# Gram correction of a cross-attention kernel in 9 instead of 12 matmuls per group

## The chip, the cores and the metric

The kernel runs on one core of one Trainium2 chip. The metric is the device time of one execution in microseconds (us), taken as the median of several runs. The core has five engines with queues of their own: TensorE (PE, matrix products), VectorE (DVE), ScalarE (ACT), GpSimd (POOL) and SyncE (SP, which issues DMAs). They meet only at semaphores.

## The reference, cut to what matters

```python
B, S, C = 8, 112, 320; H, Dh = 20, 16          # batches, queries, channels; heads
text, ip = ctx[:, :371], ctx[:, 371:]          # 371 text tokens and 4 image tokens of 512 values
q = heads(x @ W_q); k = heads(text @ W_k); v = heads(text @ W_v)
P = softmax(q k^T / 4)                         # (8, 20, 112, 371)
text_out = P v
qsem = l2norm(P @ text)                        # a vector of 512 per head and query
sem  = qsem @ l2norm(ip)^T
p_ip = softmax(q k_ip^T / 4 + 0.5 * sem) * mask
out  = (text_out + p_ip v_ip) @ W_out + b_out + x
```

The length of `P @ text` is never computed over the 512 values. With G = text text^T (371 x 371) its square is p^T G p, so the kernel needs, for all 20 heads and 112 queries of a batch, the product of G with the exponentials. All of it must come out in float32 quality, while TensorE is run in a fast 32-bit mode ("f32r") that rounds its operands. So an operand is split into a high part that survives the rounding and a low part that holds the rest, and both are multiplied.

## The kernel before, in words

**Tiles.** The 371 text tokens are three blocks of 128, 128 and 115. A batch has five groups of four heads, 40 groups in all; a group's exponentials are three tiles of 128 x 448 (tokens by 4 x 112 queries).

**One batch's own work on TensorE** (units of the order): `K` c: the keys, three pieces, 12, 12 and 8 matmuls. `G` i: block row i of G, that is the diagonal block and what is to the right of it, 12 matmuls each of 376, 248 or 120 columns. `V` j: the values, 12 matmuls each. `max` h (`m`): one matmul of scores with queries on the partitions, for the maximum over tokens by head. `mT`: the 20 maxima, transposed; they go through DVE and three small DMAs back to the queries (`qst`), and `St` of the next batch waits for those.

**Work per group g.** `St` g c (`S0`, `S1`, `S2`): scores of block c into `P`; ScalarE takes the exponential into `big` and then a rounded copy of it into `er`. `gram` g j (`g2`, `g1`, `g0`, together `g`): G times `er` for block column j into `Y`, i from 0 to j, each with a matmul of the high part `Gh` and one of the low part `Gl`: 6 + 4 + 2 = 12 matmuls of 448 columns. The blocks above the diagonal are stored doubled, so that those below can be left out (p^T G p is symmetric). DVE multiplies each `Y` with the exponentials into `pb`, POOL adds the three up. `pv` g (`v`): exponentials times values, and the sum over tokens of those products.

**Buffers that set the order.** `Y` has two banks. Its three uses per group alternate, so `g0` can start only when DVE has multiplied `g2` of the same group (semaphore `s_P`). All of `K`, `G`, `V`, `max`, `mT`, `T`, `pT`, `cT`, `o` write into a ring `PR` of three banks: the n-th such unit waits until the (n-3)-th is read (`s_free0` to `s_free2`, which count for each bank what DVE or ScalarE have read). Where a unit `max` waits in DVE's queue, its bank and TensorE's third unit behind it wait too.

**What sets the order.** `master_schedule` writes one list of units by hand; every engine walks the same list and takes from it what concerns it, DVE through `behind`, which moves some units behind the next maximum or product. `ROUNDS` holds the five rounds in which batch b's groups run beside batch b+1's `K`, `G`, `V` and maxima; `EARLY` is the same for batch 0 and `LAST` for batch 7.

Before, a `G` unit goes: ScalarE copies the diagonal block and, times 2, the rest into `Gh` (L658, L661) and the four image columns into `Vt` (L665); DVE subtracts to get `Gl` (L799, L801), which frees the bank. All matmuls but transposes carry line L905.

## Time and profile before

| | |
|---|---|
| median of 3 runs | 412.04 us (411.01 to 414.87) |
| the profiled execution, its own time | 411.41 us |
| its span, first to last instruction | 409.6 us |
| TensorE busy | 393.6 us, 96% of the span |
| VectorE busy | 220.2 us, 54% |
| ScalarE busy | 206.0 us, 50% |
| GpSimd busy | 206.3 us, 50% |
| TensorE clock granted, mean | 0.997 of full speed |

Matmuls overlap in the records: each is shown from its first column in to its last column out, so a row's duration is longer than the time for which it holds the engine. That time is the distance between the starts of two rows.

### The profile page before, as it was taken

How to read it: one execution, taken by the hardware profiler on the slowest of the kernel's cores; microseconds unless marked ns; L12 is line 12 of the kernel's file. 1: busy time of each engine (PE TensorE's matmuls, PEld its weight loads, DVE VectorE, ACT ScalarE, POOL GpSimd, SP SyncE). 2: the span in 40 equal slices, each digit the busy share in tenths (PEclk: the TensorE clock that was granted, in tenths of full speed). 3: DMA queues.
4: the chain of work that ended last, by engine and by line, in shares of the span. 5: the costliest groups of instructions: out<-in, count | busy, mean ns of one | idle time of the engine just before them, and what ended most of it. 6: DMA issues, size and time to landing. Idle time of an engine off the chain costs nothing.

```text
span 409.6 us, 9494 instructions
## 1 busy us (share of the span) xinstructions
PE 393.6 (96%) x3653; PEld 319.5 (78%) x3653; DVE 220.2 (54%) x482; ACT 206.0 (50%) x484; POOL 206.3 (50%) x218
## 2 busy tenths in 40 slices
PE   7999799899899999999999999999999999999995
PEld 4648688678788878888789878887888878876762
DVE  0795764575267534665366526663556646643432
ACT  1534134555645565555556564456455366458722
POOL 3020361262527872576437662687247443844981
PEclk9999999999999999999999999999999999999998
DMA  8499994338204802273207511470208210001000
GB/s 259 140 292 234 213 172 84 92 126 166 75 2 150 145 14 72 75 161 61 82 6 193 97 49 36 146 144 18 72 2 168 51 40 2 3 3 39 3 16 15
DMA packets 29455, 38.03 MB, mean 93 GB/s; under 512 B 14361, under 2 KB 26745, under 8 KB 28729
## 3 DMA queue, kind: packets, MB, share of 16 engines
q1 hardware_dynamic: 28514, 36.36, 37.0%
q10 hardware_dynamic: 896, 1.07, 0.9%
q8 instruction: 29, 0.48, 0.5%
q14 instruction: 16, 0.13, 0.1%
HBM read 28.50 MB, written 8.81 MB: 91 GB/s over the span
## 4 chain that ended last, share of the span: by engine, by line
PE 88%; DVE 3%; ACT 2%; issue 2%; DMA 2%; POOL 1%; POOLq 0%; SPq 0%; ACTq 0%; DVEq 0%
PE PR L905 42%; PE Y L905 27%; PE P L905 10%; PE O L905 8%; DMA pb<-wq 1%; DVE big L773 1%; PE PR L1063 1%; ACT big L681 1%; ACT er L685 1%; POOL pb L547 1%; DVE mx L807 1%; DMA qst<-ma 0%; POOLq L169 0%; SPq L460 0%; ACT cTs L729 0%
## 5 line engine op out<-in xcount | busy, mean ns | idle before, releaser
L547 POOL TENSOR_TENSOR pb<-pb 128x448 f32<-128x448 f32 x78 | 89.1, 1142 | 110.4 <-DVE pb L829 104.9
L807 DVE TENSOR_REDUCE mx<-PR 112x1 f32<-112x371 f32 x160 | 83.7, 540 | 78.1 <-PE PR L905 77.1
L905 PE MATMUL Y<-er,Gh 128*128 128x448 f32 x240 | 95.3, 397 | 1.7 <-ACT er L685 0.8
L829 DVE TENSOR_TENSOR pb<-big,Y 128x448 f32<-128x448 f32 x120 | 72.6, 621 | 39.2 <-PE Y L905 39.0
L905 PE MATMUL Y<-er,Gl 128*128 128x448 f32 x240 | 87.3, 364 | 0.0
L681 ACT ACTIVATE big<-P 128x448 f32<-128x448 f32 x120 | 65.2, 543 | 18.7 <-PE P L905 17.9
L685 ACT ACTIVATE er<-big 128x448 fp32r<-128x448 f32 x120 | 69.3, 578 | 3.8
L905 PEld LDWEIGHTS Y<-er,Gh 128*128 128x128 f32 x240 | 45.1, 188 | 13.7 <-DVE pb L829 9.1
L905 PE MATMUL PR<-kst,qst 96*112 96x371 bf16 x160 | 51.3, 331 | 2.2 <-DVE mx L807 2.0
L905 PEld LDWEIGHTS Y<-er,Gl 128*128 128x128 f32 x240 | 45.2, 188 | 2.1
L905 PE MATMUL P<-qst,kst 99*128 99x112 bf16 x480 | 42.0, 214 | 1.5 <-ACT big L681 1.1
L905 PEld LDWEIGHTS P<-qst,kst 99*128 99x128 bf16 x480 | 29.8, 99 | 17.0 <-issue 8.0
L649 ACT ACTIVATE ks<-PR 128x372 bf16<-128x372 f32 (+1 forms) x24 | 10.3, 429 | 47.8 <-PE PR L905 47.2
L905 PE MATMUL PR<-wvh,eh 128*128 128x320 f32 (+1 forms) x96 | 32.3, 336 | 0.2 <-ACT Vt L673 0.2
L673 ACT ACTIVATE Vt<-PR 128x320 f32<-128x320 f32 (+1 forms) x24 | 10.6, 442 | 41.2 <-PE PR L905 41.2
L905 PE MATMUL O<-big,Vt 128*22 128x112 f32 x960 | 31.0, 262 | 0.0
L905 PE MATMUL PR<-eh 128*128 128x376 f32 (+2 forms) x96 | 29.7, 310 | 0.0
L905 PE MATMUL PR<-wvl,eh 128*128 128x320 f32 (+1 forms) x96 | 29.7, 309 | 0.0
L905 PE MATMUL PR<-wvh,el 128*128 128x320 f32 (+1 forms) x96 | 29.6, 309 | 0.0
L569 POOL TENSOR_TENSOR t<-ssq,halfm 112x20 f32<-112x20 f32 (+2 forms) x9 | 28.8, 3202 | 1.4 <-DVE ssq L845 1.3
L905 PE MATMUL PR<-eh,el 128*128 128x376 f32 (+2 forms) x96 | 28.0, 292 | 0.0
L905 PE MATMUL PR<-el,eh 128*128 128x376 f32 (+2 forms) x96 | 28.0, 292 | 0.0
(154 smaller groups left out, 653.5 us busy)
## 6 DMA issues: line engine op xcount, KB each, us to landing
et<-ctxT SPq DMA_DIRECT2D x8, 752.0 KB, 4.4
kst<-kd SPq DMA_DIRECT2D x7, 720.0 KB, 7.2
kd<-ks SPq DMA_DIRECT2D x16, 288.0 KB, 2.9
qst<-qd SPq DMA_DIRECT2D x48, 70.0 KB, 2.4
...
```

Source lines behind the costliest of these rows:

```text
L547: pool.tensor_tensor(total, total, (pz, pm)[j], ALU.add).then_inc(s_S, 1)
L569: power = pool.tensor_tensor(t1[:, hs], ssq[:, hs], halfm[:, hs], ALU.pow)
L649: act.activation(ks[:, 0, TP * c:TP * c + w], bank[:, 0:w], ACT.Copy).then_inc(s_kh, 1)
L673: act.activation(Vt[b % 2][0:r, i, :, 0:D], bank[0:r, 0:C].rearrange("p (h d) -> p h d", d=D), ACT.Copy).then_inc(s_free[seq[u] % NR], 1)
L681: act.activation(e, P[(3 * g + c) % 2][:, 0:448], ACT.Exp).then_inc(s_exp, 1)
L685: act.activation(er[g % 2][:, 448 * c:448 * c + 448], e, ACT.Copy).then_inc(s_er, 1)
L773: dve.tensor_tensor(kblk[0:w, c, :, :].rearrange("p b (h n) -> p b h n", n=NIP), src, m, ALU.mult).then_inc(s_kb, 1)
L807: dve.tensor_reduce(mx[b % 2][:, h:h + 1], bank[0:S, 0:T], AX.X, ALU.max).then_inc(s_free[seq[u] % NR], 1)
L829: dve.tensor_tensor((pz, pm, pa[g % 2])[j], eb[g % 3][:, 448 * j:448 * j + 448], Y[y % 2][:, 0:448], ALU.mult).then_inc(s_P, 1)
L905: return pe.matmul(o, st, mv, start=start, stop=stop, **kw)
L1063: last = pe.transpose(bank[0:S, 128 * (r - lo):128 * (r - lo) + 128], OT[b % 2][:, r, :], ident[:, :])
```

## The change

G is no longer stored as it is. With c the diagonal element of a token's row and 1/c its reciprocal, row i of the stored matrix is divided by c, and the exponential's copy `er` is multiplied by c (ScalarE, `scale=gc`). Of a diagonal block only the half above the diagonal is kept, twice, with 1/2 (times 2) on the diagonal, which is exact after the division. The low parts of that upper half are transposed on TensorE (new unit `D` i, L1031) and put below the diagonal of the same block of `Gh`. So a diagonal block needs one matmul per product where it had two, 5 + 3 + 1 = 9 for a group. `Gl` is left for the blocks right of the diagonal.

DVE's part of a `G` unit is now a chain of six instructions that wait for each other (L828 to L834: diagonal, its lower bound, reciprocal, upper half, its remainder, remainder times c), then `Gl` once ScalarE has copied the rest (L841), and one more (L850) when the transposed piece is back. ScalarE starts on a `G` unit only behind `s_gd`, near the chain's end, and from batch 2 on it takes its part of `G` behind the next exponential (`late_g`). The bank of `G` is free after L841. `usel` is 2 instead of 1, and the DMA of the 128 x 128 identity becomes one of 128 x 384 (identity and two triangular masks), queued ahead of the image tokens' loads.

The rounds are written anew: two maxima stand between `K0` and `g` of the first, none between `S0` and `g` of the others; `V1` comes as the fourth ring unit behind the fourth group's products; the last maximum stands right before `mT`. Before batch 0, `G` and `K` of the next batch alternate.

```diff
+LOFF = (0, 256)
+TINY = 1e-30
...
-ROUNDS = ("S0 K0 m g m K1 S1 m v S2 m G0 m",
-          "S0 m g m K2 m S1 v m S2 G1 m",
-          "S0 m g2 T0 T1 g1 g0 m r0 G2 m S1 m pw v S2 m V0",
-          "Kr S0 r1 m g m V1 m S1 m m v r2 S2 mT z V2",
+ROUNDS = ("S0 K0 m m g m S1 m v S2 m K1 m G0",
+          "S0 g m S1 m v D0 S2 K2 m G1 m",
+          "S0 g m S1 T0 T1 v r0 m D1 S2 m G2 pw m V0",
+          "Kr S0 r1 g m D2 S1 m V1 m m v r2 m S2 m mT z V2",
           "p E g pT v cT S0 S1 o S2")
 EARLY = ("m S0 m K1 g m S1 m S2 m",
-         "S0 m g m S1 K2 m S2 v m m",
-         "S0 m g m S1 m v S2 V0 m m",
-         "Kr S0 m g m V1 m S1 m m v S2 mT V2",
+         "S0 m g m S1 K2 m S2 v D0 m m",
+         "S0 m g m S1 m v D1 S2 V0 m m",
+         "Kr S0 m g m D2 V1 m S1 m m v S2 mT V2",
...
-    order += [("G", 0, i) for i in range(3)] + [("K", 1, c) for c in range(3)] + [("Kr", 1)]
-    side = [("V", 0, 0), ("V", 0, 1), ("V", 0, 2)] + [("qip", b) for b in range(B)]
+    order += [u for c in range(3) for u in (("G", 0, c), ("K", 1, c))] + [("Kr", 1)]
+    side = [u for c in range(3) for u in (("V", 0, c), ("D", 0, c))] + [("qip", b) for b in range(B)]
...
-        if u[0] in ("K", "G") and u[1] >= 2:
+        if u[0] == "K" and u[1] >= 2:
             out, held = out + held, [u]
+        elif u[0] == "G":
+            out, held = out + held + [u], [("Gl",) + u[1:]]
         else:
             out.append(u)
-            if u[0] in ("max", "gram", "mT", "o"):
+            if u[0] in ("max", "gram", "mT", "o", "K"):
                 out, held = out + held, []
     return out + held
 
 
-RING = ("K", "G", "V", "T", "pT", "cT", "o", "max", "mT")
+def late_g(order):
+
+    out, held = [], []
+    for u in order:
+        if u[0] == "G" and u[1] >= 2:
+            held.append(u)
+        else:
+            out.append(u)
+            if u[0] == "St":
+                out, held = out + held, []
+    return out + held
+
+
+RING = ("K", "G", "D", "V", "T", "pT", "cT", "o", "max", "mT")
...
                 elif k == "G":
                     b, i, r = u[1], u[2], ROWS[u[2]]
-                    filled(act, u)
+                    act.wait_ge(s_gd, 3 * b + i + 1)
                     if b == 0:
                         act.wait_ge(s_set, FILLS)
                     if b >= 2:
                         act.wait_ge(s_gram, 3 * NG * (b - 1))
-                    a = min(128, T - 128 * i)
-                    act.activation(Gh[b % 2][0:r, GOFF[i]:GOFF[i] + a], bank[0:r, 0:a], ACT.Copy)
-                    rest = T - 128 * i - a
+                    rest = T - 128 * i - r
                     if rest:
-                        act.activation(Gh[b % 2][0:r, GOFF[i] + a:GOFF[i] + a + rest], bank[0:r, a:a + rest],
-                                              ACT.Copy, scale=2.0)
+                        act.activation(Gh[b % 2][0:r, GOFF[i] + r:GOFF[i] + r + rest], bank[0:r, r:r + rest],
+                                       ACT.Copy, scale=grc[b % 2][0:r, i:i + 1])
                     if b >= 2:
                         act.wait_ge(s_pv, NG * (b - 1))
...
-                    act.activation(er[g % 2][:, 448 * c:448 * c + 448], e, ACT.Copy).then_inc(s_er, 1)
+                    act.activation(er[g % 2][:, 448 * c:448 * c + 448], e, ACT.Copy,
+                                   scale=gc[g // NG % 2][:, c:c + 1]).then_inc(s_er, 1)
...
+                        dve.wait_ge(s_mk, 16)
+                    if b >= 2:
+                        dve.wait_ge(s_gram, 3 * NG * (b - 1))
+                    filled(dve, u)
+                    c, rc = gc[b % 2][0:r, i:i + 1], grc[b % 2][0:r, i:i + 1]
+                    low, diag = dj[i][0:r, 0:r], Gh[b % 2][0:r, GOFF[i]:GOFF[i] + r]
+                    link(dve.scalar_tensor_tensor(low, bank[0:r, 0:r], 1.0, ident[0:r, 0:r], ALU.mult, ALU.mult, accum_out=c))
+                    link(dve.tensor_scalar(c, c, TINY, None, ALU.max))
+                    link(dve.reciprocal(rc, c))
+                    link(dve.scalar_tensor_tensor(diag, bank[0:r, 0:r], rc, half_upper[0:r, 0:r], ALU.mult, ALU.mult))
+                    dve.scalar_tensor_tensor(low, bank[0:r, 0:r], rc, diag.bitcast(f32), ALU.mult, ALU.subtract).then_inc(s_gd, 1)
+                    dve.wait_ge(s_gd, 3 * b + i + 1)
+                    dve.scalar_tensor_tensor(low, low, c, upper[0:r, 0:r], ALU.mult, ALU.mult).then_inc(s_ru, 1)
+                elif k == "Gl":
+                    b, i, r = u[1], u[2], ROWS[u[2]]
+                    n = seq[("G", b, i)]
+                    o, rest = GOFF[i], T - 128 * i - r
                     dve.wait_ge(s_gh, 3 * b + i + 1)
-                    gh, gl = Gh[b % 2], Gl[b % 2]
-                    a = min(128, T - 128 * i)
-                    rest = T - 128 * i - a
-                    o = GOFF[i]
-                    low = dve.tensor_tensor(gl[0:r, o:o + a], bank[0:r, 0:a], gh[0:r, o:o + a].bitcast(f32), ALU.subtract)
                     if rest:
-                        low = dve.scalar_tensor_tensor(gl[0:r, o + a:o + a + rest], bank[0:r, a:a + rest], 2.0,
-                                                       gh[0:r, o + a:o + a + rest].bitcast(f32), ALU.mult, ALU.subtract)
-                    low.then_inc(s_free[seq[u] % NR], 1)
+                        dve.scalar_tensor_tensor(Gl[b % 2][0:r, LOFF[i]:LOFF[i] + rest], PR[n % NR][0:r, r:r + rest],
+                                                 grc[b % 2][0:r, i:i + 1], Gh[b % 2][0:r, o + r:o + r + rest].bitcast(f32),
+                                                 ALU.mult, ALU.subtract).then_inc(s_free[n % NR], 1)
+                    else:
+                        dve.sem_inc(s_free[n % NR], 1)
+                elif k == "D":
+                    b, i, r = u[1], u[2], ROWS[u[2]]
+                    filled(dve, u)
+                    diag = Gh[b % 2][0:r, GOFF[i]:GOFF[i] + r]
+                    dve.scalar_tensor_tensor(diag, bank[0:r, 0:r], grc[b % 2][0:r, i:i + 1], diag.bitcast(f32), ALU.mult,
+                                             ALU.add).then_inc(s_free[seq[u] % NR], 1)
...
+                elif k == "D":
+                    b, i, r = u[1], u[2], ROWS[u[2]]
+                    pe.wait_ge(s_ru, 3 * b + i + 1)
+                    if b == 0 and i == 0:
+                        pe.wait_ge(s_mk, 16)
+                    pe.transpose(bank[0:r, 0:r], dj[i][0:r, 0:r], ident[0:r, 0:r]).then_inc(s_ring, 1)
...
-                        freed(pe, seq[("G", b, 2)])
+                        for i in range(3):
+                            freed(pe, seq[("D", b, i)])
                     if j == 2:
                         pe.wait_ge(s_er, 3 * g + 3)
                     d = Y[y % 2][:, 0:448]
                     for i in range(j + 1):
                         o = GOFF[i] + 128 * (j - i)
                         mv = er[g % 2][:, 448 * i:448 * i + 448]
-                        mm(d, Gh[b % 2][:, o:o + 128], mv, i == 0, False)
-                        last = mm(d, Gl[b % 2][:, o:o + 128], mv, False, i == j)
+                        last = mm(d, Gh[b % 2][:, o:o + 128], mv, i == 0, i == j)
+                        if i < j:
+                            o = LOFF[i] + 128 * (j - i - 1)
+                            mm(d, Gl[b % 2][:, o:o + 128], mv, False, False)
                     last.then_inc(s_gram, 1)
                 elif k == "pv":
                     g = u[1]
```

**DVE, batch 2 on, second round.** What DVE does between the maximum (`mx`) ahead of the second `G` unit and the group's first two products (`pb`). Before:

```order
L807 TENSOR_REDUCE mx<-PR 112x1 [waits s_ring]
L799 TENSOR_TENSOR Gl<-PR,Gh 128x128 [waits s_gh]
L801 SCALAR_TENSOR_TENSOR Gl<-PR,Gh 128x115
L807 TENSOR_REDUCE mx<-PR 112x1 [waits s_ring]
L829 TENSOR_TENSOR pb<-big,Y 128x448 [waits s_pv,s_gram]
```

Now:

```order
L828 SCALAR_TENSOR_TENSOR dj,gc<-PR,masks 128x128 [waits s_kres,s_ring,s_gram]
L829 TENSOR_SCALAR gc<-gc 128x1 [waits s_d]
L830 RECIPROCAL grc<-gc 128x1 [waits s_d]
L831 SCALAR_TENSOR_TENSOR Gh<-PR,grc,masks 128x128 [waits s_d]
L832 SCALAR_TENSOR_TENSOR dj<-PR,grc,Gh 128x128 [waits s_d]
L834 SCALAR_TENSOR_TENSOR dj<-dj,gc,masks 128x128 [waits s_gd]
L855 TENSOR_REDUCE mx<-PR 112x1 [waits s_ring]
L841 SCALAR_TENSOR_TENSOR Gl<-PR,grc,Gh 128x115 [waits s_gh]
L877 TENSOR_TENSOR pb<-big,Y 128x448 [waits s_pv,s_gram]
```

Two instructions for `G` have become seven, and all seven stand ahead of the first product.

**TensorE, batch 2 on, fourth round,** from the last product of the group (the `Y` row that waits for `s_P`) to the second `V` unit. Before:

```order
L905 MATMUL Y<-er,Gh 128x448 [waits s_P]
L905 MATMUL Y<-er,Gl 128x448
L905 MATMUL PR<-kst,qst 112x371 [waits s_free2]
L905 MATMUL PR<-wvh,eh 128x320 [waits s_free0]
```

Now:

```order
L953 MATMUL Y<-er,Gh 128x448 [waits s_P]
L953 MATMUL PR<-kst,qst 112x371 [waits s_free2]
L1031 MATMUL PR<-masks,dj 115x115 [waits s_ru,s_free0]
L953 MATMUL P<-qst,kst 128x112 [waits s_exp]
L953 MATMUL P<-qst,kst 128x112 x3
L953 MATMUL PR<-kst,qst 112x371 [waits s_free1]
L953 MATMUL PR<-wvh,eh 128x320 [waits s_free2]
```

`V` (the row with `wvh,eh`) now needs bank 2, which the maximum right behind the products fills; before it needed a bank that was filled ahead of them.

**TensorE, the end of the fourth round,** from the third of the scores to the transpose of the maxima (`mx`). Before:

```order
L905 MATMUL P<-qst,kst 128x112 [waits s_exp]
L905 MATMUL P<-qst,kst 128x112 x3
L1000 MATMUL PR<-ident,mx 20x112 [waits s_free0,s_free1]
L905 MATMUL PR<-wvh,eh 115x320 [waits s_free2]
```

Now:

```order
L953 MATMUL P<-qst,kst 128x112 [waits s_exp]
L953 MATMUL P<-qst,kst 128x112 x3
L953 MATMUL PR<-kst,qst 112x371 [waits s_free0]
L1055 MATMUL PR<-masks,mx 20x112 [waits s_free0,s_free1]
L953 MATMUL PR<-wvh,eh 115x320 [waits s_free2]
```

One maximum has moved between the scores and the transpose that needs it.

## Rows read from the trace of the kernel before

**Rows 1.** The page: busy time, share of span, instructions; chain that ended last.

```profile
PE 393.6 (96%) x3653; PEld 319.5 (78%) x3653; DVE 220.2 (54%) x482; ACT 206.0 (50%) x484; POOL 206.3 (50%) x218
...
PE 88%; DVE 3%; ACT 2%; issue 2%; DMA 2%; POOL 1%; POOLq 0%; SPq 0%; ACTq 0%; DVEq 0%
PE PR L905 42%; PE Y L905 27%; PE P L905 10%; PE O L905 8%; DMA pb<-wq 1%; DVE big L773 1%; PE PR L1063 1%; ACT big L681 1%; ACT er L685 1%; POOL pb L547 1%; DVE mx L807 1%; DMA qst<-ma 0%; POOLq L169 0%; SPq L460 0%; ACT cTs L729 0%
```

**Rows 2.** Timeline of TensorE, one group's products: start us, us, instruction [idle before].

```profile
200.26 0.50 PE L905 MATMUL Y<-er,Gh 128*128 128x448 f32 x1
200.60 0.36 PE L905 MATMUL Y<-er,Gl 128*128 128x448 f32 x1
...
201.40 0.36 PE L905 MATMUL Y<-er,Gl 128*128 128x448 f32 x1
...
202.48 0.47 PE L905 MATMUL Y<-er,Gh 128*128 128x448 f32 x1
202.79 0.36 PE L905 MATMUL Y<-er,Gl 128*128 128x448 f32 x1
202.99 0.32 PE L905 MATMUL PR<-kst,qst 96*112 96x371 bf16 x1
```

**Rows 3.** Timeline of DVE, the same group.

```profile
200.59 0.54 DVE L807 TENSOR_REDUCE mx<-PR 112x1 f32<-112x371 f32 x1 [2.12 <-PE PR L905]
201.06 0.53 DVE L780 TENSOR_TENSOR kr<-PR,ks 128x372 f32<-128x372 f32 x1
201.80 0.62 DVE L829 TENSOR_TENSOR pb<-big,Y 128x448 f32<-128x448 f32 x1 [0.21 <-PE Y L905]
202.60 1.21 DVE L829 TENSOR_TENSOR pb<-big,Y 128x448 f32<-128x448 f32 x2 [0.17 <-PE Y L905]
```

**Rows 4.** Chain of waits in order of time: start us, us, what, instructions.

```profile
205.74 0.90 PE O L905 x32
...
218.94 0.54 PE PR L1063 x5
...
228.63 2.08 PE PR L905 x14
```

**Rows 5.** Timeline of DVE, instructions that do and don't wait for each other.

```profile
37.51 0.28 DVE L799 TENSOR_TENSOR Gl<-PR,Gh 128x128 fp32r<-128x128 f32 x1
37.71 0.40 DVE L801 SCALAR_TENSOR_TENSOR Gl<-PR,Gh 128x243 fp32r<-128x243 f32 x1
...
233.07 0.26 DVE L815 SCALAR_TENSOR_TENSOR mr<-PR,ma 20x112 f32<-20x112 f32 x1
233.37 0.20 DVE L817 CAST ma<-mr 20x112 bf16<-20x112 f32 x1
```

**Rows 6.** Timeline of ScalarE around a `G` unit.

```profile
217.57 0.25 ACT L665 ACTIVATE Vt<-PR 128x80 f32<-128x80 f32 x1
217.69 0.56 ACT L681 ACTIVATE big<-P 128x448 f32<-128x448 f32 x1
218.28 0.58 ACT L685 ACTIVATE er<-big 128x448 fp32r<-128x448 f32 x1
...
225.71 0.44 ACT L673 ACTIVATE Vt<-PR 128x320 f32<-128x320 f32 x1 [0.77 <-PE PR L905]
```

**Rows 7.** Timeline before batch 0, DVE.

```profile
35.80 1.79 DVE L747 TENSOR_TENSOR el<-et,eh 128x752 fp32r<-128x752 f32 x2 [2.61 <-ACT eh L630]
...
46.18 3.96 DVE L773 TENSOR_TENSOR big<-kipT,hq 128x640 f32<-128x640 f32 x3
```

**Rows 8.** Timeline before batch 0, TensorE.

```profile
50.64 0.81 PE L905 MATMUL PR<-kst,qst 96*112 96x371 bf16 x2 [1.84 <-DVE mx L807]
...
62.80 0.36 PE L905 MATMUL PR<-kst,qst 96*112 96x371 bf16 x1
63.89 0.26 PE L1000 MATMUL PR<-ident,mx 112*20 112x112 f32 x1 [0.73 <-DVE mx L807]
```

**Rows 9.** Busy time by stretch: PE, PEld, DVE, ACT, POOL, clock, DMA share, GB/s.

```profile
4.00:8.00 4.00, 2.67 (x11) 2.04 (x10) 0.00 (x0) 0.16 (x1) 0.70 (x6) 1.00 0.99 277
...
405.00:409.60 4.60, 1.03 (x3) 0.39 (x3) 0.49 (x1) 0.26 (x1) 0.00 (x0) 0.77 0.10 31
```

30 lines of the change are left out of this document (22 added, 8 removed).

## The prediction, made before the changed kernel ran

> **What bounds the kernel now.** I read the page first: TensorE is busy 96% of the span and the chain that ended last is TensorE to 88%, of which the products into `Y` are 27% [rows 1]. So matmuls taken out should shorten it, unless TensorE then waits instead. The next view is the timeline of one group's products on TensorE [rows 2] beside DVE's [rows 3]. Matmuls follow at 0.20 us (200.60 to 201.40 is four steps), so twelve would take 2.40 us. The block takes 2.59: from its effective start at 200.40 to 202.99. The missing 0.19 is one stall: the third product (`g0`) starts at 202.48 because the multiply that empties its `Y` bank ran 201.80 to 202.42. TensorE is already at the edge of waiting for DVE inside each group, although DVE is busy only 54%. The reader should keep one number from here: the distance from the last `g2` matmul's start (201.40) to the release of `g0` (202.42) is 1.02 us, all DVE and latency, and the change doesn't shorten it.
>
> **Matmuls removed.** 40 groups lose 3 of 12. With 5 + 3 + 1, the last `g2` matmul starts 0.20 earlier, so DVE's multiply ends at 202.22 and `g0` starts at 202.28; it is one matmul, and the next unit starts 0.31 later (202.48 to 202.79 [rows 2]), at 202.59 instead of 202.99. A group gains 0.40 us, not 0.60: a third goes into a longer wait for `Y`. 40 x 0.40 = 16.0; in batch 7 the scores stand between the products and cover some 0.1 of the wait in each of 5 groups: **-16.5 us**.
>
> **Transposes added.** 24 `D` units. Five transposes of 128 x 128 take 0.54 us on the chain [rows 4], 0.11 each: **+2.6 us**.
>
> **DVE's chain for a `G` unit.** No row has it, so I bound it. Instructions that wait for each other start 0.30 us apart for 0.26 of work; two that don't start 0.20 apart for 0.28 [rows 5]. The chain is six: four on a 128 x 128 tile, two on a column. Lower end: all at 0.20, 1.2 us. Upper end: all at 0.32, 1.9. I take 1.55 (four at 0.29, two at 0.20), nearest the rows that wait. The Trainium skill (VectorE: DVE Perf Modes, The DRAIN you can't avoid) says that a semaphore between two DVE instructions costs nothing extra. By that rule the chain would be near 1.2 and the sum some 5 us lower; the rows above speak against it.
>
> What this costs depends on what stands behind it. I walked batch 4's five rounds in the new order, with these steps: maximum 0.16 us on TensorE and 0.46 on DVE (200.59 to 201.06 [rows 3]), multiply 0.60, `pv` 0.90 [rows 4], `V` 1.76 (2.08 less two maxima [rows 4]), scores 0.20, exponential and copy together 1.15 on ScalarE [rows 6]. Let the products start at S; DVE must have multiplied `g2` by S+1.82.
>
> - Round 1: DVE has two maxima and `K`'s remainder (3 x 0.46) at its queue's head when the products start, and comes 0.2 late. **0.2 us.**
> - Round 2: `G0` ends 0.2 before S, DVE's chain runs S+0.0 to S+1.5, the multiply ends at S+2.1. **0.3.** (Chain 1.2: nothing.)
> - Round 3: `G1` and a maximum end 0.2 before S; DVE does the chain to S+1.4, the maximum to S+1.85, `Gl` to S+2.05, then the multiply to S+2.65. **0.8.** (Chain 1.2: 0.5; 1.9: 1.15.)
> - Round 4, ScalarE: it takes `G2` behind the exponential of `S0`, and DVE's multiply stands behind `s_gh`. `V0` ends at S-0.2; ScalarE does `Vt` (0.44), exponential and copy (1.15), then 0.25 [rows 6], done near S+1.7; the multiply ends at S+2.3. **0.5**, whatever the chain takes.
> - Round 4, ring: behind the products come maximum, `D2`, scores, maximum, `V1`, and `V1` needs the first one's bank. Let X be the end of the `g2` multiply. TensorE is there at X+1.0 (0.37 to leave `g0`, 0.16, 0.11, 0.20, 0.16). DVE first does two multiplies (1.2), then the maximum (0.54): X+1.8. **0.8.** Before, `V1` used a bank filled ahead of the products.
> - Round 4, the last maximum: it stands right ahead of `mT`. From a maximum's start to such a transpose's start is 1.09 us where nothing else is between (62.80 to 63.89 [rows 8]; the chain puts it at 1.02 behind the matmul's own start-up), against 0.16 for the maximum. **0.85.** Before, `pv` and the scores lay between.
> - Round 5: nothing new, **0**.
>
> 3.45 us in each of batches 1 to 6, the rounds that carry `G` and `D`: **+20.7 us**. In batch 0's rounds `G` is done before and `V1` waits for an older bank: only the gains above.
>
> **Before batch 0.** (a) `K` of batch 1 now stands second, but DVE's split of its context ends at 37.59 (35.80 + 1.79 [rows 7]), while `G0` ends near 35.9: TensorE idles 1.65 us. (b) In the alternation the fourth unit needs `G0`'s bank, which is free after chain 1.55, ScalarE's 0.6, and, on DVE, `K`'s remainder and `Gl`: about 1.3 more for both such places, less what (a) covered, so the first `V` starts 2.9 us late. (c) DVE then builds a block of 3.96 us [rows 7]. Before, `V1` ran beside it and TensorE idled 1.84 [rows 8]; now a third maximum stands ahead of `V1`, the ring is full earlier, and V1's 1.76 come behind: +1.2 net of the later start. Together **+4.1**. (d) Batch 1's three `G` units follow on each other with three chains (4.65 us) and three `Gl`; here ScalarE takes `G` in the old place, so the first exponential waits about 2.9 us longer, and the first products start 2.0 later: **+2.0**.
>
> **Costed at nothing.** The mask DMA moves 128 KB more, 0.5 us at the 277 GB/s of its stretch [rows 9], ahead of image-token loads that are used near 30 us. Three small fills on POOL lie before any use; POOL's sums wait for DVE anyway. ScalarE's copies keep their count and size (the scale comes from a column); if that costs 0.05 each, 6 us on an engine half idle. The way of the maxima from `mT` to the next scores takes 5.0 us; between them stand `V2`, the products, `pv` and, in batches 1 to 4, `cT`: 5.5 us or more, so it stays hidden by half a microsecond.
>
> **Sum.** -16.5 + 2.6 + 20.7 + 6.1 = +12.9. Of this I take 2 off: the chain has 2% "issue" [rows 1], 8 us of small gaps, some of which lie under the new waits. The profiled execution took 411.4 us, 0.6 under the median of 412.0; so 412.0 + 10.9 = **423 us**.
>
> **Rivals.**
> 1. *DVE keeps up and the matmuls' time is collected: faster.* One mechanism: at each group TensorE's queue holds work that needs neither the ring nor `Y`, and the waits I found vanish. For it: DVE has 190 us idle now and gets about 40 more of work; the new rounds put the scores and two maxima elsewhere. Against: the listed places are fixed orders in a ring of three. It decides by one number: the fixed parts sum to -16.5 + 2.6 + 6.1 = -7.8, so below 1.3 us of waits in a batch it is faster, above it slower. With 0.5 a batch: 412 - 7.8 + 3 = 407 us; without the prologue's delay 402. Chance of more than 1% faster: 0.14.
> 2. *Half of the waits.* With a chain of 1.2 us and the round-1 and round-2 waits gone, or the ring's wait halved, 1.7 to 2 us a batch are left and 4 before batch 0: 412 - 13.9 + 4 + 11 = 413 us. Chance 0.20.
> 3. *TensorE's clock falls too.* In the last 4.6 us TensorE is busy 1.03 and the granted clock's mean is 0.77 [rows 9], so between its levels of 2.4 and 1.2 GHz; before batch 0 it idled 1.84 us and stayed at 1.00. I expect a pause of 3.3 us at that place. If the clock halves behind it for a few microseconds of work, +3: 427 us. The Trainium skill (TensorE: Matmul & The Clock Gate, HAM oscillation) says that pauses between bursts put the array back to its half rate; the trace shows it at the end only. Together with a chain of 1.9 us (+3 to 5): up to 431. Chance 0.12.
> 4. *The forecast,* 418 to 427 us: 0.54.
>
> About 1% is what a measurement of this kernel can tell from no change. Faster by over 1% (under 407.9): 0.14. Within 1%: 0.20. Slower by over 1% (above 416.2): 0.66. The range 408 to 429 leaves out rival 1 and the upper tail of rival 3.
>
> **What would show it.** `Y` matmuls 360 instead of 480, `g0` starting 0.06 us behind the end of the `g2` multiply in every group. DVE's chain at 1.2 to 1.9 us. In the table of waits TensorE's weight loads or matmuls into `PR` behind the maxima's line, in total near 10 us, where now the ring hardly shows; TensorE's waits for DVE's multiplies near 20 us. A pause between the first `V` and the second before batch 0. TensorE busy under 90%. I am wrong if `V1` of the fourth round follows its maximum without a pause, or if the chain on DVE is under 0.9 us.

## The result: 9% slower, and more than forecast

| | before | changed |
|---|---|---|
| median of 4 runs each, same chip | 413.46 us (411.01 to 415.57) | 450.34 us (447.78 to 452.34) |
| profiled execution: time, span | 411.41, 409.6 us | 447.78, 446.0 us |
| TensorE busy | 393.6 us, 96% | 390.1 us, 87% |
| VectorE busy | 220.2 us, 54% | 260.5 us, 58% |
| TensorE clock granted, mean | 0.997 | 0.984 |

Ratio 1.089, 95% interval 1.079 to 1.099. The forecast was 423 us with a range of 408 to 429: the side was right, the size was not. Of about 37 us more, 11 were forecast.

The page of the changed kernel, in answer to [rows 1]: busy times, then the chain that ended last.

```profile
PE 390.1 (87%) x3557; PEld 306.4 (69%) x3557; DVE 260.5 (58%) x650; ACT 214.8 (48%) x460; POOL 205.4 (46%) x220
...
PE 62%; DVE 19%; issue 6%; POOL 5%; ACT 4%; DMA 2%; POOLq 0%; SPq 0%; ACTq 0%; DVEq 0%
PE PR L953 37%; PE Y L953 11%; PE P L953 7%; PE O L953 6%; DVE pb L877 6%; DVE mx L855 4%; POOL pb L576 2%; POOL t L598 1%; ACT big L708 1%; DVE dj L832 1%; DVE Gh L831 1%; DMA pb<-wq 1%; DVE dj L828 1%; DVE kr L808 1%; DVE big L801 1%
```

Three things are to be seen. TensorE's busy time fell by only 3.5 us although 120 of its matmuls went (run 1 below, which removes just them, stands at 378.9): the row of a matmul behind a wait is longer (0.48 against 0.37 us below), and so are rows at the lower clock (0.51 against 0.33 for `K`'s). VectorE has 168 instructions more and 40 us more of work, yet is busy 58%. And it has gone from 3% to 19% of the last chain. No engine is full; the engines wait for each other in turn.

The table of waits gives the sums behind that. Columns: engine and line that waits, what it waits for, us in all, times, the longest.

```profile
PE Y L953 <- DVE pb L877: 23.1, 24, 1.9
PE PR L953 <- DVE mx L855: 7.1, 12, 2.5
PE PR L1055 <- DVE mx L855: 5.6, 7, 0.8
```

The first is TensorE waiting for a `Y` bank, once in each of 24 groups, 0.5 to 1.9 us (shorter waits are not in this table); the second the ring; the third `mT` behind the last maximum, once a batch.

**Where the 36.4 us lie.** I take the start of each group's first product from both timelines. Until group 0 starts (75.34 before, 85.29 now) 9.95 are lost, of 6.1 forecast. Batch 0's groups give 0.4 back, and batch 7's with the end 1.4. The six batches between cost 28.2, 4.7 each. Batch 3 stands for them. The table holds its five rounds, each from one group's first product to the next one's, at full clock (where a kernel further below had a fall of the clock in one, its neighbour batch's same round is taken).

| kernel, batch 3 | r1 | r2 | r3 | r4 | r5 | sum |
|---|---|---|---|---|---|---|
| before | 9.18 | 7.99 | 8.32 | 8.57 | 10.51 | 44.57 |
| `b9` (9 matmuls, nothing else) | 8.96 | 7.74 | 7.73 | 8.18 | 10.11 | 42.72 |
| changed | 9.10 | 8.11 | 10.66 | 10.81 | 10.29 | 48.97 |
| changed less `b9` | 0.14 | 0.37 | **2.93** | **2.63** | 0.18 | 6.25 |
| forecast, waits and `D` | 0.2 | 0.41 | 0.91 | 2.26 | 0 | 3.78 |

Four rounds came within 0.4 of the forecast. The third did not.

**The third round, row by row.** TensorE's timeline of the changed kernel, batch 3 (start us, us, instruction, idle before). It answers to [rows 2].

```profile
237.23 0.45 PE L953 MATMUL Y<-er,Gh 128*128 128x448 f32 x1
...
238.73 0.37 PE L953 MATMUL Y<-er,Gh 128*128 128x448 f32 x1
240.99 0.48 PE L953 MATMUL Y<-er,Gh 128*128 128x448 f32 x1 [1.89 <-DVE pb L877]
241.30 0.32 PE L953 MATMUL PR<-kst,qst 96*112 96x371 bf16 x1
...
243.20 0.37 PE L953 MATMUL PR<-kst,qst 96*112 96x371 bf16 x1
243.64 0.33 PE L1031 MATMUL PR<-masks,dj 128*128 128x128 f32 x1
243.81 0.36 PE L953 MATMUL P<-qst,kst 99*128 99x112 bf16 x4
244.01 0.32 PE L953 MATMUL PR<-kst,qst 96*112 96x371 bf16 x1
244.52 0.31 PE L953 MATMUL PR<-eh 128*115 128x120 f32 x1 [0.19 <-DVE mx L855]
```

The products take 4.07 us (237.23 to 241.30) where nine matmuls need about 2.3. Then `D1` starts 0.44 behind a maximum that holds TensorE for 0.16, and `G2` 0.51 behind one. VectorE in the same stretch, in answer to [rows 3, 5]:

```profile
237.17 0.29 DVE L828 SCALAR_TENSOR_TENSOR dj<-PR,masks 128x128 f32<-128x128 f32 x1 [0.65 <-PE PR L953]
237.39 0.08 DVE L828 DVE_READ_ACCUMULATOR dj<-PR,masks 128x1 f32 x1
237.51 0.15 DVE L829 TENSOR_SCALAR gc<-gc 128x1 f32<-128x1 f32 x1
237.70 0.16 DVE L830 RECIPROCAL grc<-gc 128x1 f32<-128x1 f32 x1
237.90 0.35 DVE L831 SCALAR_TENSOR_TENSOR Gh<-PR,grc,masks 128x128 fp32r<-128x128 f32 x1
238.28 0.35 DVE L832 SCALAR_TENSOR_TENSOR dj<-PR,grc,Gh 128x128 f32<-128x128 f32 x1
238.67 1.04 DVE L834 SCALAR_TENSOR_TENSOR dj<-dj,gc,masks 128x128 f32<-128x128 f32 x1
239.63 0.53 DVE L855 TENSOR_REDUCE mx<-PR 112x1 f32<-112x371 f32 x1
240.09 0.32 DVE L841 SCALAR_TENSOR_TENSOR Gl<-PR,grc,Gh 128x115 fp32r<-128x115 f32 x1
240.33 1.79 DVE L877 TENSOR_TENSOR pb<-big,Y 128x448 f32<-128x448 f32 x3
```

The chain starts 0.06 before the products (0.15 was forecast). It ends not at S+1.4 but at S+2.48, and the first multiply runs S+3.10 to S+3.70 instead of ending at S+2.65. The 1.05 us of difference are 0.1 of start, 0.3 of length and 0.66 of one instruction, L834. It takes 1.04 us here, and 0.34 in the next unit (247.51 for 115 x 115, not shown); of 24 such units five are so slow. These five lie in the third rounds of batches 1 to 5. Each time GpSimd has this instruction running (timeline of GpSimd):

```profile
237.69 1.88 POOL L567 TENSOR_TENSOR ks<-kr,ks 128x954 bf16<-128x954 f32 x1
```

It ends at 239.57, L834 at 239.71. Batch 6 has no such instruction of GpSimd in its third round. There L834 takes 0.35 and the round 9.97 us instead of 10.66.

### The profile page after: what moved, and what is told of

The parts are those of the page before. It is cut to its first block, busy times and chain, and to the rows that moved or that the text cites. A ratio compares the mean times of both kernels' runs of the same rounds, so it can differ in the third digit from the quotient of the medians.

```text
span 446.0 us, 9507 instructions
## 1 busy us (share of the span) xinstructions
PE 390.1 (87%) x3557; PEld 306.4 (69%) x3557; DVE 260.5 (58%) x650; ACT 214.8 (48%) x460; POOL 205.4 (46%) x220
## 4 chain that ended last, share of the span: by engine, by line
PE 62%; DVE 19%; issue 6%; POOL 5%; ACT 4%; DMA 2%; POOLq 0%; SPq 0%; ACTq 0%; DVEq 0%
PE PR L953 37%; PE Y L953 11%; PE P L953 7%; PE O L953 6%; DVE pb L877 6%; DVE mx L855 4%; POOL pb L576 2%; POOL t L598 1%; ACT big L708 1%; DVE dj L832 1%; DVE Gh L831 1%; DMA pb<-wq 1%; DVE dj L828 1%; DVE kr L808 1%; DVE big L801 1%
## 5 line engine op out<-in xcount | busy, mean ns | idle before, releaser
L855 DVE TENSOR_REDUCE mx<-PR 112x1 f32<-112x371 f32 x160 | 82.5, 537 | 55.5 <-PE PR L953 54.0
L953 PE MATMUL Y<-er,Gh 128*128 128x448 f32 x240 | 89.3, 398 | 25.4 <-DVE pb L877 23.1
L877 DVE TENSOR_TENSOR pb<-big,Y 128x448 f32<-128x448 f32 x120 | 71.1, 616 | 31.5 <-PE Y L953 30.0
L712 ACT ACTIVATE er<-big,gc 128x448 fp32r<-128x448 f32 x120 | 80.3, 670 | 3.9
L953 PEld LDWEIGHTS P<-qst,kst 99*128 99x128 bf16 x480 | 31.5, 100 | 18.4 <-issue 7.1
L953 PE MATMUL Y<-er,Gl 128*128 128x448 f32 x120 | 44.1, 368 | 0.0
L953 PE MATMUL O<-big,Vt 128*22 128x112 f32 x960 | 32.0, 268 | 0.0
L953 PEld LDWEIGHTS PR<-kst,qst 96*112 96x112 bf16 x160 | 20.6, 132 | 10.3 <-issue 4.4
L953 PEld LDWEIGHTS O<-big,Vt 128*22 128x22 f32 x960 | 21.7, 103 | 7.7 <-issue 7.0
```

The source lines that it names most:

```text
L712: act.activation(er[g % 2][:, 448 * c:448 * c + 448], e, ACT.Copy, scale=gc[g // NG % 2][:, c:c + 1]).then_inc(s_er, 1)
L855: dve.tensor_reduce(mx[b % 2][:, h:h + 1], bank[0:S, 0:T], AX.X, ALU.max).then_inc(s_free[seq[u] % NR], 1)
L877: dve.tensor_tensor((pz, pm, pa[g % 2])[j], eb[g % 3][:, 448 * j:448 * j + 448], Y[y % 2][:, 0:448], ALU.mult).then_inc(s_P, 1)
L953: return pe.matmul(o, st, mv, start=start, stop=stop, **kw)
```

## The experiments

Runs 1, 2, 3 and 16 edit the kernel before, the others the changed one. Where a run leaves work out, its result is not the reference's; it only tells times. Ratios are to runs of the kernel before on the same chip. Times of rounds are those of batch 3.

**1. Only the matmuls removed.** The kernel before without its diagonal low parts.

```diff
-                        mm(d, Gh[b % 2][:, o:o + 128], mv, i == 0, False)
-                        last = mm(d, Gl[b % 2][:, o:o + 128], mv, False, i == j)
+                        last = mm(d, Gh[b % 2][:, o:o + 128], mv, i == 0, i == j)
+                        if i < j:
+                            mm(d, Gl[b % 2][:, o:o + 128], mv, False, False)
```

> The kernel before with the matmul of the diagonal blocks' low parts left out (9 matmuls per group, all else as it was; the diagonal's low part is left out of the result). Theory 1, removed matmuls are worth 0.40 us a group because g0 waits for its Y bank: 40 x 0.40 = 16 us less, ratio 0.96, and a group's products take 2.2 us instead of 2.6. Theory 2, they are worth their 0.20 us each: 24 us less, ratio 0.94, 2.0 us a group. Theory 3, TensorE is paced by others: less than 8 us.

400.87 us, ratio 0.968 (0.963 to 0.973). A batch gains 1.85 us, 0.37 a group, where I had 0.40. The full 0.60 isn't there, since a third turns into waiting for `Y`. So the gain was sized rightly. The whole kernel gains 12.9 us and not 14.8: its profile shows a granted clock of 0.78 over 78 to 84 us and of 0.79 over 104 to 112, where the kernel before stands at 1.00.

**2. Work between the products.** `b9` with scores, a maximum or `K2` between `g1` and `g0` (first round `S0 K0 m g2 g1 S1 g0 m K1 ...`).

> As b9, and a unit that needs neither Y nor DVE (scores, a maximum or pT) stands between g1 and g0 of nearly every group. If the wait for the Y bank is what eats a third of the gain, g0 comes some 0.2 us less late and the kernel is 5 to 8 us faster than b9 (ratio to before 0.94). If b9 gains its full 24 us, this changes nothing.

398.17 us, 0.964 (0.956 to 0.972), 2.7 less than `b9` where 5 to 8 were expected. A batch falls from 42.72 to 42.25: 0.47 of the 1.15 us that went into `Y` waits comes back.

**3. Only the new order,** with twelve matmuls and the old arithmetic (`ROUNDS` and `EARLY` of the change without `D`).

> The kernel before, 12 matmuls, with the changed kernel's five rounds and early rounds (without D units). Theory 1, the moves cost 0.8 us at V1 and 0.85 at the maximum ahead of mT, in each of six batches: 10 us slower, ratio 1.025. Theory 2, the moves are harmless and all of the loss is DVE's chain and what it delays: within 1% of before.

420.34 us, 1.016 (1.011 to 1.022); 45.95 us a batch, 1.38 more than before, of which 1.10 in round 4 (9.67 against 8.57). That is the ring's wait at `V1` and the maximum ahead of `mT`, priced at 1.65 with nine matmuls. The order costs by itself, though less than the 10 us expected. Its third round is only 0.15 longer than before (8.47 against 8.32).

**4. Only the new arithmetic, old rounds.** `ROUNDS` as before, each `D` a round later than its `G`.

> The changed kernel with the five rounds of before, D units put in behind (the prologue and the early rounds stay changed). Theory 1, V1 and mT are 10 us of the loss: about 440 us. Theory 2, the chain is what costs, wherever the maxima stand: about 448 us. Third case, the old rounds put the chain at a worse place (maxima between S0 and g wait behind it): above 452 us.

442.47 us, 1.068 (1.063 to 1.073); rounds 8.97, 9.32, 10.46, 8.34, 10.11. Round 4 is nearly that of `b9`, but rounds 2 and 3 take 1.6 and 2.7 more. In either order about 2.8 us sit in round 3. The arithmetic brings that, not the order. The parts differ, though: here L834 takes 0.62 to 0.63 in six third rounds, each time ending 0.14 behind another instruction of GpSimd (`tn`, 0.72 us).

**5. The slow last instruction.** L834 reads its block from PSUM again, so one of its two tensors lies in SBUF and not both. (The low part that is transposed is then not the right one.)

```diff
-                    dve.scalar_tensor_tensor(low, bank[0:r, 0:r], rc, diag.bitcast(f32), ALU.mult, ALU.subtract).then_inc(s_gd, 1)
+                    link(dve.scalar_tensor_tensor(low, bank[0:r, 0:r], rc, diag.bitcast(f32), ALU.mult, ALU.subtract))
+                    dve.scalar_tensor_tensor(low, bank[0:r, 0:r], c, upper[0:r, 0:r], ALU.mult, ALU.mult).then_inc(s_gd, 1)
                     dve.wait_ge(s_gd, 3 * b + i + 1)
-                    dve.scalar_tensor_tensor(low, low, c, upper[0:r, 0:r], ALU.mult, ALU.mult).then_inc(s_ru, 1)
+                    dve.sem_inc(s_ru, 1)
```

> The changed kernel, with the last instruction of DVE's chain reading PSUM instead of its first SBUF operand (one SBUF operand instead of two; the transposed low part is then not the right one). In the changed kernel's trace this instruction takes 0.35 us 19 times and 1.01 to 1.04 us 5 times, each time while GpSimd's 1.9 us subtraction of bf16 keys (L567) runs, in the third round of batches 1 to 5. Theory 1, two SBUF operands wait for GpSimd's instruction to end: none is over 0.4 us now, the third round's products take 3.4 instead of 4.06 us, 0.7 us a batch, 3 to 4 us in all (near 445 us). Theory 2, it is the write or the access as such: the 1.03 us stay.

447.07 us, 1.081 (1.075 to 1.086). The instruction takes 0.35 us in all places. GpSimd's 1.88 us and the instruction in the same stretch (VectorE, then GpSimd, from run 11, which has the same edit):

```profile
237.47 0.35 DVE L833 SCALAR_TENSOR_TENSOR dj<-PR,gc,masks 128x128 f32<-128x128 f32 x1
```

```profile
236.49 1.88 POOL L567 TENSOR_TENSOR ks<-kr,ks 128x954 bf16<-128x954 f32 x1
```

So the mechanism is shown: with both tensors in SBUF the instruction stands until GpSimd's ends; with one in PSUM it runs beside it. The Trainium skill (SBUF — State Buffer, SBUF: two separate sides) states this, that such an instruction of VectorE and one of GpSimd that reads SBUF take one pair of ports in turn and the loser is fully blocked. The traces agree, 0.35 against 1.04 us. But round 3 falls only from 10.66 to 10.20 and round 2 grows by 0.3, because ScalarE's start was moved behind one more link. Batch 6, where nothing is held, shows that cost alone: its round 3 rises from 9.97 to 10.21. Of the 0.66 us, 0.16 a batch is left (48.97 to 48.81).

**6. Half the chain.** No diagonal, bound or reciprocal: three instructions (c = 1).

> The changed kernel without the diagonal's extraction, its bound and the reciprocal (three of six instructions of DVE's chain; the scaling is left out, the factors are 1). The chain falls from 1.85 us to 1.1. Theory 1, each of the chain's parts that is in the way costs its full length in the second and third round (0.3 and 0.75 us a batch) and in the three chains before batch 0 and before its first group (0.7 each): 8 to 10 us less than the changed kernel, near 440. Theory 2, what counts is that the chain exists and ScalarE waits for it: under 4 us less.

444.56 us, 1.075 (1.068 to 1.082), where near 440 was the first expectation. Round 2 falls to 7.58, round 3 stays at 10.63. The held instruction explains that. In this kernel it is L832 and starts earlier, but GpSimd's instruction ends no earlier (VectorE, then GpSimd, batch 3 of this run):

```profile
232.74 1.76 DVE L832 SCALAR_TENSOR_TENSOR dj<-dj,gc,masks 128x128 f32<-128x128 f32 x1
```

```profile
232.48 1.87 POOL L568 TENSOR_TENSOR ks<-kr,ks 128x954 bf16<-128x954 f32 x1
```

It takes 1.76 us now instead of 1.04 and again ends 0.15 behind GpSimd's. What the chain loses in front is waited for behind. In batch 6, where nothing is held, another path is next: round 3 falls from 9.97 to only 9.70, since VectorE's `Gl` then waits for ScalarE, whose part of `G` stands behind an exponential and its copy.

**7. G copied at once** (`late_g` left out).

```diff
-            for u in late_g(order):
+            for u in order:
```

> The changed kernel, with ScalarE taking its part of G in its old place (late_g left out, nothing else). Theory 1, in the fourth round DVE's first multiply waits for ScalarE's copies, which stand behind the exponential of S0: its products then take 2.4 instead of 2.9 us, and the second and third round stay, since they wait for the chain itself: 3 us less, near 447. Theory 2, ScalarE is held up for 1.5 us by every chain, the exponentials come late, and products wait for er: slower than the changed kernel.

446.45 us, 1.079 (1.073 to 1.085). Round 4 falls by 0.60 (10.81 to 10.21), the wait for `s_gh` that I had at 0.5. Round 3 stays: there the chain holds it, and ScalarE's part was never the later one.

**8. The maxima of round 4 put back,** so that `V1` finds its bank and a maximum stands further ahead of `mT`.

```diff
-          "Kr S0 r1 g m D2 S1 m V1 m m v r2 m S2 m mT z V2",
+          "Kr S0 r1 m g m D2 V1 m S1 m m m v r2 S2 mT z V2",
```

> The changed kernel with one string of the rounds changed: in the fourth round a maximum stands again between S0 and g, D2 and V1 behind the one after it, and no maximum stands between the last scores and mT. Theory 1, the ring and the late maximum cost 0.8 + 0.85 us in each of six batches: the fourth round takes 9.2 instead of 10.8 us, 10 us less in all, near 440. Theory 2, they only show what DVE owes anyway, and it comes back later: the batch keeps its 49.0 us.

449.17 us, 1.086 (1.080 to 1.091), a miss. Round 4 does fall, by 2.19 to 8.62. But round 3 rises by 1.91. TensorE reaches the maximum that now precedes the products and waits for the bank of `G2`, which ScalarE reads only behind that group's exponential. Timelines of TensorE (scores, then the maximum) and of ScalarE (the last copy from that bank) in this kernel:

```profile
249.70 0.37 PE L953 MATMUL P<-qst,kst 99*128 99x112 bf16 x4
251.71 0.36 PE L953 MATMUL PR<-kst,qst 96*112 96x371 bf16 x1 [1.63 <-DVEq L845]
```

```profile
251.38 0.22 ACT L692 ACTIVATE Vt<-PR 115x80 f32<-115x80 f32 x1
```

The maximum starts 0.11 behind the end of the copy. The changed kernel's order and `late_g` belong together: with G copied late, no maximum can stand there.

**9. Both together** (7 and 8).

> ring_fix and g_at_once together. ring_fix took 2.2 us out of the fourth round (10.8 to 8.6) and put 1.9 us on the third (10.7 to 12.6). Theory 1, the 1.9 us are the bank of G2: the maximum between S0 and g is the third ring unit behind it, and the bank is free only when ScalarE has done the exponential of S0 and then its part of G2. With ScalarE's part at once the third round is back at 10.7 or below and the fourth at 8.6: 46.8 us a batch instead of 49.0, near 436 us. Theory 2, DVE owes those 2 us wherever the maxima stand: 48.5 us or more a batch.

438.67 us, 1.060 (1.058 to 1.062); 46.84 us a batch. This undoes 2.1 of the change's 6.25 a batch. It settles round 4: ring, last maximum and ScalarE, together 2.2 where 2.15 were forecast.

**10. One instruction instead of six.** Five of the chain left out, so neither diagonal, reciprocal nor low part is made.

> The changed kernel with one instruction of 0.35 us in place of DVE's chain of six (nothing of the diagonal, its factor or its low part is computed; orders, D units, waits of ScalarE and all matmuls stay). In the order of before the full arithmetic costs 47.2 us a batch against 42.7 in b9. Theory 1, it is the chain: without it the second and third round fall by 0.5 and 1.9 us (chain and the wait for GpSimd), the fourth by nothing (there ScalarE's exponential is in the way): 46.5 us a batch instead of 49.0, and the first products start at 80 us instead of 85: about 428 us. Theory 2, it is the D units, the added waits and the fuller ScalarE: 48 us or more a batch.

435.77 us, 1.054 (1.050 to 1.057); round 3 is 9.70, as in batch 6 of run 6. Near 428 us was expected. Now `Gl` starts 0.17 behind the end of ScalarE's copy, which still stands behind the exponential: chain and ScalarE's late copy had to go together.

**11, 12. The paths of round 3 apart and together.** 9 with 5, and 9 with 10.

> The changed kernel with three edits together: ring_fix (the maxima of round 4 in an order that lets V1 start), ScalarE's G copy at once and not behind exp, and the chain's last instruction reading its block from PSUM so that it has one SBUF operand. In ring_fix_at_once rounds 3 and 4 of batch 3 take 10.71 and 8.60 us and the whole kernel 438.7 us. If the waits of round 3 add (the theory), the 0.66 us of the slow last instruction come off it: round 3 at 9.8 to 10.2 us, 46 to 46.4 us a batch, 434 to 437 us. If another path stands beside it (ScalarE's copies), round 3 stays at 10.5 to 10.7 and the kernel at 438 to 440 us.

436.80 us, 1.057 (1.052 to 1.063); 47.04 us a batch. The products of round 3 shrink by 0.45, but the round stays at 10.63 (10.71 in run 9). TensorE gives it back at the round's end, as its timeline shows: the bank of `G2` comes free only when chain and ScalarE are through, and this edit starts ScalarE one link later. Batch 6, where nothing is held, shows the price: its round 3 is 10.64 here and 10.04 in run 9. So the held instruction did cost some 0.66, and the edit that removes it costs 0.60.

```profile
246.04 0.37 PE L954 MATMUL P<-qst,kst 99*128 99x112 bf16 x4
246.57 0.36 PE L954 MATMUL PR<-kst,qst 96*112 96x371 bf16 x1 [0.15 <-DVEq L846]
```

```profile
246.22 0.24 ACT L692 ACTIVATE Vt<-PR 115x80 f32<-115x80 f32 x1 [2.42 <-DVE dj L833]
```

> As ring_fix_at_once (maxima of round 4 reordered, G copied at once), and the chain of six VectorE instructions cut to one of 0.35 us: the five that extract the diagonals, bound and scale them are left out, so the matrix is not the reference's. If chain and G copy are the two parallel paths of round 3, both are gone: the start of round 3 to 4 falls from 10.7 to 9.0 to 9.6 us, about 44.7 us a batch, 424 to 428 us. If the added transpose units and VectorE's queue cost by themselves, round 3 stays at 9.7 or more, 45.3 us a batch or more, 429 to 432 us.

418.16 us, 1.012 (1.008 to 1.016), below the 424 expected; 9.10, 7.57, 8.92, 8.65, 10.30, sum 44.54. VectorE and TensorE of its third round:

```profile
225.07 0.35 DVE L831 SCALAR_TENSOR_TENSOR Gh<-PR,grc,masks 128x128 fp32r<-128x128 f32 x1 [0.65 <-PE PR L952]
225.56 0.54 DVE L854 TENSOR_REDUCE mx<-PR 112x1 f32<-112x371 f32 x1
226.02 0.33 DVE L840 SCALAR_TENSOR_TENSOR Gl<-PR,grc,Gh 128x115 fp32r<-128x115 f32 x1
226.43 1.80 DVE L876 TENSOR_TENSOR pb<-big,Y 128x448 f32<-128x448 f32 x3
```

```profile
225.13 0.45 PE L952 MATMUL Y<-er,Gh 128*128 128x448 f32 x1
...
227.41 0.32 PE L952 MATMUL PR<-kst,qst 96*112 96x371 bf16 x1
```

The products take 2.28 us, against 4.05 in run 9, and the round is shorter by the same 1.79. This settles the larger part of the third round: 1.77 of its 2.93 are the chain ahead of the multiplies. Batch 6 splits it. With nothing held its round 3 takes 10.04 in run 9 and 8.94 here: 1.10 are the chain's own length, and 0.67 (10.71 less 10.04) the wait for GpSimd. The remaining 1.19 (8.92 against 7.73 in `b9`) is in the next section. The run also bounds the idea in this order. With five of the six instructions gone a batch is back at 44.54, just where the kernel before stands (44.57), and the work ahead of batch 0 is still 8.9 us longer (84.23 against 75.34).

**13. Before batch 0 as it was:** the three `G` and then the three `K`, the `D` behind the `V`; DVE frees `G` of batch 0 at once.

> The changed kernel with the work before batch 0 in the order of before (three G, three K, three V, then the D units spread over the maxima; Gl right behind its G). In the changed kernel the first group's products start at 85.3 us, before at 75.3. Theory 1, 1.3 us are K's wait for the context's split and 1.8 V1's place behind the 3.9 us block: they start at 82 us, and 6.5 us are left, which are the chains (three before batch 0, three ahead of the first exponential). Theory 2, the chains alone set it, and it stays at 85.

452.66 us, 1.094 (1.092 to 1.096), another miss. The stretch in question ends earlier in it (the first `qip` at 55.67 against 59.93, 53.36 before), so the alternation delayed most of it. But the clock takes more than that back (columns: stretch and length, busy PE, PEld, DVE, ACT, POOL with counts, granted clock, DMA share, GB/s):

```profile
54.00:64.00 10.00, 9.79 (x47) 7.84 (x47) 5.41 (x14) 2.38 (x6) 7.24 (x3) 0.65 0.99 167
64.00:75.00 11.00, 10.27 (x38) 8.66 (x38) 3.88 (x10) 0.95 (x4) 1.67 (x1) 0.50 0.14 24
```

**14, 15. Orders meant to be better.** `tuned1`: new rounds, `G` of batch 0 spread among other work, `Gl` behind the multiplies, G copied at once. `tuned2`: new rounds and G copied at once, nothing else.

> The changed arithmetic in an order made for its chain: each G unit has pv or V behind it on TensorE while DVE does the chain, ScalarE takes G at once, Gl goes behind a product's multiply, scores or a maximum stand between g1 and g0, no maximum stands right ahead of mT, G1 comes 3.5 us behind K2 (GpSimd's subtraction is over), batch 0's G0 is put ahead of vip, its three V run beside the 3.9 us block, and batch 1's G units stand in batch 0's rounds behind K of batch 2. Theory 1, the loss is the chain's places and not its length: 42.5 to 43 us a batch as in b9_fill and 400 to 405 us. Theory 2, DVE's added 40 us of work are too much wherever they stand: 415 us or more.

446.02 us, 1.076 (1.068 to 1.085), where 400 to 405 was the hope. A batch takes 46.33, the least of all with the whole arithmetic, but ahead of batch 0 the clock stands at 0.50 for 64 to 75 us in this one too, and it falls again in the third rounds of batches 2 and 4 (13.01 us each instead of 9.89). L834 takes 0.35 us in all 24 places here and in run 15: an order can keep it off GpSimd's time.

> The changed kernel with new strings for the five rounds alone and ScalarE's part of G at once: pv behind G0 and G1, V0 behind G2, so that the chain runs beside them; scores between g1 and g0; maxima in ones and twos between long units, none right ahead of mT; K2 early enough that GpSimd's subtraction is over at G1. Theory 1, the chain costs little where TensorE has 1.8 us of work that needs neither ring nor Y behind each G: 43.5 to 44.5 us a batch, 25 us less than the changed kernel, near 422 (the 10 us before batch 0 stay). Theory 2, DVE's queue is too full for any order (tuned1 had 46.3 us a batch): 46 us or more, above 435.

436.77 us, 1.057 (1.052 to 1.062), 46.76 a batch, where near 422 was the hope: as good as run 9 by another way. With nothing held, round 3 still takes 9.39.

**16. The filler with all twelve matmuls,** the order of run 2 in the kernel before.

> The kernel before, 12 matmuls, with only the order of b9_fill: scores, a maximum or pT between g1 and g0. In before g0 waits 0.09 us for its Y bank and loses 0.1 more to the late weight load in 35 groups. Theory 1, this is taken away: 0.15 x 35 = 5 us faster, ratio 0.988. Theory 2, the moves that make the room cost as much: ratio 0.995 to 1.005.

412.71 us, 0.996 (0.994 to 0.999). That is the one kernel here that does the whole computation and is not slower than before; the gain is 1.0 us between the medians and 1.5 by the ratio, hardly more than the measurement tells.

## Why the side was right and the size wrong

*Matmuls removed, -16.5:* a tenth too much. 1.85 a batch in run 1, 14.8 in 40 groups.

*Round 1, round 2, round 5:* right within 0.2 each.

*Round 4, 2.15:* right in sum and in its parts. Run 7 shows 0.60 for ScalarE (0.5 forecast). The timeline of TensorE shows the other two, `V1` and the transpose of the maxima:

```profile
251.26 0.32 PE L953 MATMUL PR<-kst,qst 96*112 96x371 bf16 x1
252.13 0.42 PE L953 MATMUL PR<-wvh,eh 128*128 128x320 f32 x1 [0.55 <-DVE mx L855]
...
255.70 0.32 PE L953 MATMUL PR<-kst,qst 96*112 96x371 bf16 x1
256.85 0.26 PE L1055 MATMUL PR<-masks,mx 112*20 112x112 f32 x1 [0.82 <-DVE mx L855]
```

0.87 from the maximum to `V1` less its own 0.16 is 0.7 (0.8 forecast); 1.15 before `mT` less 0.16 is 1.0 (0.85).

*Round 3: the step that failed.* It had "DVE does the chain to S+1.4 ... then the multiply to S+2.65. 0.8". The mechanism was right, the term mis-sized, and a second one was not seen. What the runs put in its place, for the 2.93:

- Chain, 1.77 (run 12 against run 9), where 0.8 stood. Six linked instructions take 1.85 from the first start to the last end (237.17 to 239.02, with L834 at 0.35), not 1.55: linked tensors start 0.39 apart, not 0.30 ([rows 5] had no instruction with a column operand, and those take 0.35 where 0.28 was read), and an accumulator read of 0.08 comes on top. My upper bound of 1.9 was the right value. By the forecast's own walk it gives 1.15, and 1.10 was measured. The other 0.66 is L834 held by GpSimd, for which the forecast had no term.

  The kernel before shows such a wait too. [rows 7] gave three instructions of VectorE (L773, both tensors in SBUF) as 3.96 us together. Taken apart, shortest, median and longest in ns:

```profile
L773 DVE TENSOR_TENSOR big<-kipT,hq x3: 809/814/2491, 46.2 to 49.3; 128x640 f32<-128x640 f32 x2, 64x640 f32<-64x640 f32 x1
```

  The longest in VectorE's timeline, and GpSimd's instruction beside it:

```profile
46.91 2.49 DVE L773 TENSOR_TENSOR big<-kipT,hq 128x640 f32<-128x640 f32 x1
46.20 2.52 POOL L538 TENSOR_TENSOR ks<-kr,ks 128x954 bf16<-128x954 f32 x1
```

  Two take 0.81 and the one beside GpSimd's splitting of the keys takes 2.49. GpSimd's own takes 2.52 there instead of 1.88: VectorE's first L773 had started 0.02 before it, so here it was GpSimd that waited. The forecast read the sum and not the three. The page of the Trainium skill named in run 5 would have told it as well.
- The remaining 1.19, as read from traces: `T0 T1` moved out from between `g2` and `g1`, about 0.43. They fill 0.65 us of TensorE (242.30 less 241.66, timeline of TensorE). Inside the products 0.43 of that lies under the wait for `Y`: `b9` takes 2.50 for products and `T0 T1` together, run 12 takes 2.28 for the products alone, so they cost 0.22 there. I had listed the move and priced it at nothing.
- `R`, ScalarE's copy of `T0 T1`, stands behind an exponential; `D1` waits 0.28 for its bank, and `G2` 0.35 for a maximum that VectorE gives only after `rden`. Together 0.63.
- `D1` itself 0.17, and one maximum fewer in the round, -0.16. The sum is 2.84 of 2.93. No run takes these last parts away one by one, and two speak for caution: run 3 makes the same moves with twelve matmuls and its round 3 grows by only 0.15, and run 4 leaves `T0 T1` in place and its round 3 is 2.73 above `b9`. The 1.19 is measured, its split is not shown.

*Transposes, +2.6:* a `D` unit holds TensorE for 0.17 (243.64 to 243.81), so 4 us in all rather than 2.6.

*Before batch 0, +6.1:* too low, 9.95. `mT`, at 63.89 before, is at 70.06: 6.2 where 4.1 stood. Most of the difference is the clock. Windows of the changed kernel, then its timeline of TensorE:

```profile
50.00:56.00 6.00, 3.88 (x15) 3.62 (x15) 3.22 (x6) 0.06 (x1) 0.20 (x1) 0.72 0.43 126
82.00:86.50 4.50, 4.31 (x16) 4.19 (x17) 0.62 (x2) 2.22 (x4) 0.00 (x0) 0.63 0.05 13
192.00:196.00 4.00, 4.00 (x49) 3.19 (x47) 2.22 (x6) 2.82 (x7) 3.64 (x5) 0.57 0.32 82
196.00:290.00 94.00, 82.83 (x799) 67.64 (x798) 54.80 (x143) 48.09 (x102) 47.50 (x45) 1.00 0.32 76
291.00:295.00 4.00, 4.00 (x49) 3.20 (x47) 2.16 (x6) 2.90 (x7) 3.46 (x5) 0.57 0.74 170
```

```profile
52.12 0.36 PE L953 MATMUL PR<-kst,qst 96*112 96x371 bf16 x1 [2.54 <-DVE mx L855]
...
53.03 0.47 PE L953 MATMUL PR<-wvh,el 128*128 128x320 f32 x1
53.30 0.47 PE L953 MATMUL PR<-wvh,eh 128*128 128x320 f32 x1
```

Behind the pause of 2.54 us (3.3 forecast) `V1` runs with a matmul every 0.27 us instead of 0.146, at 1.2 instead of 2.4 GHz: some 1.5 us. A second fall doubles the spacing of `K`'s matmuls right ahead of the first products, some 1.0. So the 3.8 us from `mT` to the first products, with 2.0 forecast, are, as far as the trace tells, that fall and three chains of 1.85 and not 1.55. Two more falls lie in round 3 of batches 2 and 4, a little over 1 us behind the wait of 1.9 us for `Y`, where the round takes 11.53 instead of 10.66; batches 3 and 5 have the same wait and no fall. Four falls cost about 4.2 us. That was rival 3, with a chance of 0.12 and a price of 3, though it had only one such place. The trace of before had shown one fall, at its end.

*The 2 us taken off for "issue" gaps:* wrong. "Issue" went from 2% to 6% of the chain.

**The sum again,** against the 12.9 before that allowance. Ahead of batch 0: 6.1 forecast, 9.95 measured. Batches 1 to 6: 6 x (3.78 - 2.00) = 10.7 forecast, 28.2 measured; of the 17.5 between, 6 x 2.47 = 14.8 are the rounds as in the table, 1.7 two falls of the clock, and 0.9 the matmuls' gain at 1.85 instead of 2.00. Batches 0 and 7 with the end: -3.9 forecast, -1.8 measured. That makes the 36.4 us of span.

*Rivals.* DVE keeping up (0.14): excluded; every wait that I listed is in the trace. Half of the waits: excluded. *What would show it:* the chain at 1.85 and `Y`'s waits at 23.1 came as written. I wrote near 10 us for the ring's waits; 12.7 for the two lines of maxima are there.

**Still open:** how the 1.19 us of round 3 beside the chain divide, and whether the 0.63 behind `R` would go by another order; why in runs 13 and 14 the clock stayed low for 20 us while in the changed kernel each fall is short. Granted clock and busy rows show that it happens, not what sets its length.
